# Gated scores transposed and added onto the turned probabilities, sine products of both halves in one, NF4 compares in rows of 171

## What is computed

```
qs = softmax(q); ks = softmax(k); g = log_sigmoid(k) / 16
o_lin: S = S * exp(g_t) + k_t v_t^T ; o_t = q_t S        # a scan over tokens
y = softmax(rope(q) rope(k)^T / sqrt(D), window of two blocks of 64) v
o = (0.5 * y + 0.5 * o_lin).bfloat16 @ Wo
x = x + layernorm(o)
nf4(w): per block of 64, absmax; normalized = w / (1 if absmax == 0 else absmax)
        idx = searchsorted(15 bounds, normalized); CODE[idx] * absmax
h = silu(x dq(w1)^T) * (x dq(w2)^T);  x = x + layernorm(h dq(w3)^T)
```

## Time and profile before

| | |
|---|---|
| median of 3 runs | 1913.04 us (1912.93 to 1913.94) |
| the profiled execution | 1912.8 us, its span 1911.0 us |
| PE busy | 1834.3 us, 96% |
| PEld busy | 1212.8 us, 63% |
| DVE busy | 1484.2 us, 78% |
| ACT busy | 1278.5 us, 67% |
| POOL busy | 1264.8 us, 66% |
| HBM | 47 GB/s over the span |

### The profile page before, as it was taken

The page is one execution under the profiler, slowest core; times in us unless marked ns, Lnnn a source line. Parts: engine busy times, 40 slices in busy tenths (PEclk is TensorE's granted clock), DMA queues, the critical chain, the costliest instruction groups (busy, mean ns, idle before and its releaser), DMA issues.

```text
span 1911.0 us, 42834 instructions
## 1 busy us (share of the span) xinstructions
PE 1834.3 (96%) x11439; PEld 1212.8 (63%) x11439; DVE 1484.2 (78%) x3980; ACT 1278.5 (67%) x4967; POOL 1264.8 (66%) x1164
## 2 busy tenths in 40 slices
PE   4899999999999999999999999999989999999997
PEld 3567667676777677667767776776666654444443
DVE  5999899999999888899998889999999956302112
ACT  5688777777777777777777777777677745312121
POOL 2767777777777777777777777777766738212121
PEclk8999999999999999999999999999999999999999
DMA  6101111111111111111111111111211033000000
GB/s 223 54 30 44 38 50 48 46 44 46 45 45 43 43 48 43 43 43 43 43 44 50 43 43 43 43 43 35 85 31 30 24 110 111 34 1 22 0 22 22
DMA packets 85452, 90.51 MB, mean 47 GB/s; under 512 B 14216, under 2 KB 56456, under 8 KB 85384
## 3 DMA queue, kind: packets, MB, share of 16 engines
q1 hardware_dynamic: 85384, 89.71, 15.2%
HBM read 76.48 MB, written 13.18 MB: 47 GB/s over the span
## 4 chain that ended last, share of the span: by engine, by line
PE 49%; DVE 23%; issue 19%; POOL 4%; ACT 2%; DVEq 1%; DMA 0%; POOLq 0%; ACTq 0%
PE bank L1369 12%; PE bank L1398 6%; PE bank L1358 5%; DVE f_s L1061 5%; PE bank L1340 4%; PE bank L1414 4%; PE bank L1496 3%; PE bank L1407 3%; PE bank L1435 3%; DVE f_nrm L1048 2%; PE bank L1324 2%; DVE qtT L961 2%; POOL hl L600 2%; PE bank L1514 2%; DVE qc L909 2%
## 5 line engine op out<-in xcount | busy, mean ns | idle before, releaser
L554 POOL TENSOR_TENSOR f_acc<-f_acc,f_s 128x512 f32<-128x512 f32 x429 | 548.9, 1279 | 32.6 <-POOL f_acc L554 0.4
L1369 PE MATMUL bank<-wh,xh 128*128 (+2 forms) x1024 | 335.0, 327 | 7.5 <-DVE cumh L1210 6.3
L1369 PE MATMUL bank<-wl,xh 128*128 (+2 forms) x1024 | 335.0, 327 | 0.0
L1369 PE MATMUL bank<-wh,xl 128*128 (+2 forms) x1024 | 334.8, 327 | 0.0
L1061 DVE TENSOR_SCALAR f_s<-f_nrm 128x512 f32<-128x512 f32 x480 | 282.1, 647 | 3.5
L538 POOL TENSOR_TENSOR pr<-pr,rp 128x512 f32<-128x512 f32 x128 | 133.3, 1041 | 216.1 <-DVE rp L983 216.1
L651 ACT ACTIVATE qe<-bank,nqm 128x128 f32<-128x128 f32 x512 | 180.9, 365 | 95.7 <-DVE qs L912 84.0
L1496 PE MATMUL bank<-xh,w 128*128 (+3 forms) x704 | 218.4, 379 | 1.7 <-ACT sg L837 1.7
L600 POOL TENSOR_TENSOR hl<-hf,hh 128x512 f16<-128x512 f32 (+1 forms) x44 | 51.3, 1167 | 231.4 <-ACT hh L843 231.4
L1220 DVE SCALAR_TENSOR_TENSOR hf<-bank,sg 128x512 f32<-128x512 f32 (+1 forms) x44 | 30.3, 689 | 221.5 <-PE bank L1496 210.6
L1358 PE MATMUL bank<-wh,oT 128*128 (+1 forms) x512 | 194.0, 379 | 4.4 <-DVE xl L1127 3.6
(11 more groups left out here) (179 smaller groups left out, 4918.9 us busy)
## 6 DMA issues: line engine op xcount, KB each, us to landing
f_blk<-wa SPq DMA_DIRECT2D x33, 320.0 KB, 2.9
f_raw<-wb SPq DMA_DIRECT2D x33, 256.0 KB, 2.7
dequantised<-f_w SPq DMA_DIRECT2D x33, 256.0 KB, 2.0
w<-dequantised SPq DMA_DIRECT2D x33, 256.0 KB, 4.3
raw_qkv<-wq SPq DMA_DIRECT2D x29, 256.0 KB, 2.4
raw_o<-wo SPq DMA_DIRECT2D x29, 256.0 KB, 2.6
f_recb<-scales SPq DMA_DIRECT2D x99, 64.0 KB, 2.6
f_absb<-scales SPq DMA_DIRECT2D x99, 64.0 KB, 2.6
```

What stands on the lines that cost most here:

```text
L554: nc.gpsimd.tensor_tensor(f_acc[:], f_acc[:], f_s[:, step, :], ALU.add).then_inc(s["f_ad"], 1)
L1369: last = nc.tensor.matmul(dst, av, w[:, sl + c, lo:hi], start=(n == 0), stop=(n == 3 * NC - 1))
```

## The change

Six edits:

1. **Scores.** `probabilities(l2)` now stands ahead of `gla_scores(l2)` on PE, right behind `project_out`, and opens the accumulation in `X1`. `gla_scores` has no mask matmuls: it multiplies with the keys as the stationary operand, so that the scores come out transposed, and adds them onto the turned probabilities, in two f32 matmuls of 256 columns. The first of them (queries 0 to 63 of the tile) needs only the first 64 keys; they are in a new tile `ktF`, whose other columns stay zero, and ACT's `copy_ktT` writes it with one more instruction, behind a wait for the scores of the tile before.
2. **Mask.** `cau` is now 0 or 1; `merge` is one product of the bank with `cau`, straight into `pa`. `copy_pa` on ACT is gone, and DVE's `merge` stands behind `add_out`.
3. **State.** The product `em` on DVE and its semaphore are gone; ACT's `decays` makes `em` with one exponential of one column, with a bias of 0 or -1e30, in turns with p = 0 of the tile.
4. **Sine.** `rope` has one sine product over both halves, read from the bank in reversed order of the halves.
5. **NF4.** `f_s` has rows of 171 columns at a pitch of 172; `f_nrm` and `f_acc` have 3 x 171 = 513 columns without a gap. The zero-maximum guard `f_safe` is gone: each block has a 65th column with the smallest normal number, so the maximum is never zero.
6. **`nf4_end`** stands behind `p_max` instead of ahead of `gla_k`. So POOL's first addition of a piece, which waits for it, and ACT's `nf4_high`, which is queued ahead of `p_exps`, are released later.

Around it: two more memsets on DVE at the start, `cum` moves into the space of `f_s`, and the block maxima's load is 65/64 as long.

```
-                half = lambda a: a.rearrange("p (h n) -> p h n", h=GRP)[:, 0:2, 0:WIN]
-                nc.tensor.matmul(half(X1[:]), identb[:], half(cau[:]), start=True, stop=False)
-                nc.tensor.matmul(X1[:, 2 * P:], identb[:], cau[:, 2 * P:], start=False, stop=False)
...
+                for b, keys in enumerate((ktF[:], ktT[:, r, :])):
+
+                    last = nc.tensor.matmul(X1[:, b * 256:(b + 1) * 256], keys,
+                                            qtT[:, r, b].rearrange("p h n -> p (h n)"),
+                                            start=False, stop=(b == 1), skip_group_check=True)
...
 def probabilities(t):
-                wait_tile(pe, s["pm_d"], t)
+                wait_tile(pe, s["pn_p"], t)
+                wait_tile(pe, s["pa_ev"], t, 1)
                 for j in range(GRP):
-                    last = nc.tensor.transpose(X1[:, j * P:(j + 1) * P], pr[:, r, j * P:(j + 1) * P], ident[:])
+                    last = nc.tensor.matmul(X1[:, j * P:(j + 1) * P], pr[:, r, j * P:(j + 1) * P], ident[:],
+                                            start=(j == 0), stop=False, is_transpose=True, skip_group_check=True)
...
 def merge(t):
-                nc.vector.scalar_tensor_tensor(out=half(v), in0=half(X1[:]), scalar=0.0, in1=half(v),
-                                               op0=ALU.max, op1=ALU.add)
-                nc.vector.scalar_tensor_tensor(out=v[:, 2 * P:], in0=X1[:, 2 * P:], scalar=0.0, in1=v[:, 2 * P:],
-                                               op0=ALU.max, op1=ALU.add).then_inc(s["pm_d"], 1)
+                nc.vector.tensor_tensor(pa[:, t.p % 2, :], X1[:], cau[:], ALU.mult).then_inc(s["pa_ev"], 1)
...
 def copy_ktT(t):
                 wait_tile(act, s["ktT_done"], t)
+                wait_tile(act, s["at_done"], t, 1)
+                nc.scalar.activation(ktF[:, 0:WIN], SM[:, 0:WIN], ACT.Copy)
                 nc.scalar.activation(ktT[:, t.p % 2, :], SM[:, 0:P], ACT.Copy).then_inc(s["ktT_ev"], 1)
...
-                nc.vector.tensor_tensor(d4[:, :, 0, :], s4[:, :, 1, :], sin_b(t, 0, n), ALU.mult)
-                nc.vector.tensor_tensor(d4[:, :, 1, :], s4[:, :, 0, :], sin_b(t, 1, n), ALU.mult).then_inc(done, 1)
+                nc.vector.tensor_tensor(d4, s4[:, :, ::-1, :], sin_b(t, n), ALU.mult).then_inc(done, 1)
...
-                    nc.vector.tensor_scalar(f_s[:, k % 8, :], f_nrm[:], float(BOUND[k]), float(DELTA[k]),
+                    nc.vector.tensor_scalar(step_rows(k % 8), in_rows(f_nrm[:]), float(BOUND[k]), float(DELTA[k]),
                                             ALU.is_gt, ALU.mult).then_inc(s["f_sd"], 1)
...
-                    nc.gpsimd.tensor_tensor(f_acc[:], f_acc[:], f_s[:, step, :], ALU.add).then_inc(s["f_ad"], 1)
+                    nc.gpsimd.tensor_tensor(in_rows(f_acc[:]), in_rows(f_acc[:]), step_rows(step), ALU.add).then_inc(s["f_ad"], 1)
```

More of the change, by code:

```diff
@@ L38 @@
 BLK = 64
+GUARDED = BLK + 1
+SMALLEST = float(np.finfo(np.float32).tiny)
 NF4_PIECE = 512
+NF4_ROWS = 3
+NF4_ROW = 171
 NF4_MAXIMA = 10
@@ L204, in layer @@
         ktT = sb("ktT", [P, 2, P])
+        ktF = sb("ktF", [P, P])
         krT = sb("krT", [P, 4, WIN])
@@ L218, in layer @@
         rp = sb("rp", [P, 2, GRP])
-        f_safe = sb("f_safe", [P, NF4_MAXIMA])
         PQ, PKV, X0, X1, SC, SM, PO, PW = bank
@@ L550, in add_step @@
                         pool.wait_ge(s["f_dqd"], j)
[L551 removed]
+                    nc.gpsimd.tensor_tensor(in_rows(f_acc[:]), step_rows(first), step_rows(step), ALU.add).then_inc(s["f_ad"], 1)
                 elif k > 1:
                     pool.wait_ge(s["f_ad"], j * 14 + (k - 1))
[L554 removed]
+                    nc.gpsimd.tensor_tensor(in_rows(f_acc[:]), in_rows(f_acc[:]), step_rows(step), ALU.add).then_inc(s["f_ad"], 1)
             def nf4_add(t):
@@ L664, in decays @@
                 nc.scalar.activation(edT[:, r, :], SM[:, P:P + 130], ACT.Exp)
+                if t.p == 0 and not (isinstance(t.i, int) and t.i == 0):
+                    nc.scalar.activation(em[:, 0, :], SM[:, 2 * P:2 * P + 1], ACT.Exp,
+                                         bias=keep[:].unsqueeze(2)[:, t.i % 2, :])
                 nc.scalar.activation(ked, ked, ACT.Exp, scale=-1.0).then_inc(s["dec_ev"], 1)
@@ L795, in turn @@
                         split_high(0, job, 3)
-                if l2.real():
-                    copy_pa(l2)
                 if x_tile_at(n):
@@ L865, in _ @@
             silu(0, 0)
-            copy_pa(l1)
             high_hidden(0, 0)
@@ L900, in _ @@
             nc.vector.memset(krT[:], 0.0).then_inc(s["z_id"], 1)
+            nc.vector.memset(f_nrm[:], 0.0)
             nc.vector.memset(f_col[:], 0.0).then_inc(s["z_id"], 1)
+            nc.vector.memset(ktF[:], 0.0).then_inc(s["z_id"], 1)
             cos_b = lambda t, n: cos[:, t.i % 2, t.p, :].unsqueeze(1).to_broadcast([P, n, P // 2])
-            sin_b = lambda t, half, n: sin[:, t.i % 2, t.p, half, :].unsqueeze(1).to_broadcast([P, n, P // 2])
+            sin_b = lambda t, n: sin[:, t.i % 2, t.p, :, :].unsqueeze(1).to_broadcast([P, n, 2, P // 2])
             def rope(t, src, n, dc, ds, done):
@@ L1075, in nf4_end @@
                     dve.wait_ge(s["f_lod"], j)
-                nc.vector.scalar_tensor_tensor(out=f_dq[:], in0=f_acc[:], scalar=float(CODE[0]), in1=f_absb[:],
+                nc.vector.scalar_tensor_tensor(out=f_dq[:], in0=f_acc[:, 0:NF4_PIECE], scalar=float(CODE[0]), in1=f_absb[:],
                                                op0=ALU.add, op1=ALU.mult).then_inc(s["f_dqd"], 1)
@@ L1140, in turn @@
                     q_sums(l1)
-                if t.p == 1 and not (isinstance(t.i, int) and t.i == 0):
-                    nf4_end(t.i - 1)
                 if t.p == 2 and not (isinstance(t.i, int) and t.i == 0):
@@ L1154, in turn @@
                     p_max(l1)
+                if t.p == 1 and not (isinstance(t.i, int) and t.i == 0):
+                    nf4_end(t.i - 1)
                 log_decay(t)
@@ L1330, in gla_scores @@
                 wait_tile(pe, s["ktT_ev"], t)
-                wait_tile(pe, s["pa_ev"], t, 1)
-                half = lambda a: a.rearrange("p (h n) -> p h n", h=GRP)[:, 0:2, 0:WIN]
-                nc.tensor.matmul(half(X1[:]), identb[:], half(cau[:]), start=True, stop=False)
-                nc.tensor.matmul(X1[:, 2 * P:], identb[:], cau[:, 2 * P:], start=False, stop=False)
-                for b in range(2):
-                    keys = (b + 1) * WIN
-                    for hp in range(2):
-                        j = 2 * b + hp
-                        last = nc.tensor.matmul(X1[:, j * P:j * P + keys],
-                                                qtT[:, r, b, 2 * hp:2 * hp + 2, :].rearrange("p h n -> p (h n)"),
-                                                ktT[:, r, 0:keys], start=False, stop=(j == 3))
+                for b, keys in enumerate((ktF[:], ktT[:, r, :])):
+                    last = nc.tensor.matmul(X1[:, b * 256:(b + 1) * 256], keys,
+                                            qtT[:, r, b].rearrange("p h n -> p (h n)"),
+                                            start=False, stop=(b == 1), skip_group_check=True)
                 last.then_inc(s["at_done"], 1)
@@ L1588, in constants @@
     win = np.ascontiguousarray(win.reshape(P, 2, 512))
-    n = np.arange(P)[:, None] % WIN
-    cau = np.zeros((P, 2, 2, P), np.float32)
-    for b in range(2):
-        cau[:, b] = np.where(n + b * WIN >= slot, 0.0, -3e38)[:, None, :]
+    key = np.arange(P)[:, None]
+    query = np.arange(WIN)[None, :]
+    cau = np.zeros((P, 2, GRP, WIN), np.float32)
+    cau[:, 0] = ((key >= WIN) | (query >= key))[:, None, :]
+    cau[:, 1] = (query + WIN >= key)[:, None, :]
     cau = np.ascontiguousarray(cau.reshape(P, 512))
@@ L1602, in constants @@
     cum /= 16.0
-    keep = np.ones((P, 2), np.float32)
-    keep[:, 0] = 0.0
+    keep = np.zeros((P, 2), np.float32)
+    keep[:, 0] = MASKED
     return {"cosc": cos, "sinc": sin, "winmask": win, "causal": cau, "cumsum": cum,
```

78 lines of the change are left out of this document (34 added, 44 removed).

## The result

The changed kernel takes **1844.14 us** (median of 4 runs, 1843.49 to 1844.88) against 1912.99 (4 runs, 1912.75 to 1913.94) before: ratio **0.9639**, 95% interval 0.9623 to 0.9656, or 68.8 us less.

A forecast was written before the change was run, and what follows sets the result against it. PE was taken as the bound, with 60 us of stalls waiting for DVE, whose instructions wait for POOL. PE -24, steady stalls -20, start and end -10: -54, from 1912.8 to 1859 us; own range 1848 to 1868, 8-in-10 range 1845 to 1880.

The forecast's parts named there:

- PE's own work: On PE, mask matmuls removed and scores slightly cheaper: each turn 0.19 us shorter, -24 us over 127 turns.
- The stall before the scores: PE's wait for `qtT`, 0.43 us per four turns: 1.5 us of room from cheaper compares, so it goes.
- The stall before the update: PE's wait for `kt` ahead of the state update: of 0.69 us per four turns 0.25 is left.
- Start and end: Stalls in the first and last turns, 19 + 14.5 us: 30% of 34 gained, -10 us.
- The tail: What follows the turns: the forecast's sum has no term for it.
- Dearer compares elsewhere: DVE in turns with p = 0, 1, 2: compares add up to 0.5, 1.0, 1.2 us, hidden under PE.
- `em` and the merged sines: DVE: without `em` (0.87 us) `p_max` is no longer late; merged sines save 0.06 before `qtT`, 0.1 before `kt`.
- Rival A: Stalls only exchanged, through late `oT`, `ktT` or `qtT`: 1884 us, or between 1868 and 1884; chance 0.17.
- Rival B: DVE's compares still take the two-element form, 3.67 us for four: about 1862 us; counted within the forecast's chance of 0.66.
- C: More gained: no stall in steady turns, most gone at both ends, 1843 us; chance 0.10 with all below 1848.
- D: POOL becomes the bound, its additions in rows of 171 taking up to 1.93 us: about 1985 us; chance 0.05.

The follow-up runs named there:

- e7: Changed kernel with `nf4_end` back at its old place ahead of `gla_k` instead of behind `p_max`: 1854.84 us, ratio 0.9697.
- e3: Changed kernel with compares and additions on one run of 512 columns instead of rows of 171: 1884.38 us, ratio 0.985.
- e6: Changed kernel with the sine product in `rope` as two instructions again, for q and for k: 1847.48 us, ratio 0.9658.
- e15: Changed kernel with compares and additions on runs of 512, and five of POOL's additions cut to 256 columns: 1843.75 us, ratio 0.9639.
- e11: Changed kernel with one more DVE instruction in every turn, a repeated row maximum of q ahead of `rope`: 1895.20 us, ratio 0.9904.
- e5: Changed kernel with the product `em` back on DVE instead of ACT's exponential: 1844.60 us, ratio 0.9644.
- e8: Kernel before with one edit only, compares and additions in 3 rows of 171: 1904.92 us, ratio 0.9961.
- e13: Changed kernel with compares and additions on runs of 512, plus one DVE instruction ahead of the four compares in turns with p = 3: 1885.13 us, ratio 0.9853.
- e1: Kernel before with only the edits on scores and mask: 1902.18 us, ratio 0.9945.
- e10: Changed kernel with the gap in the compares' source `f_nrm`, while `f_s` and `f_acc` are without gap: 1847.98 us, ratio 0.9659.

## Why the prediction was right or wrong

The mechanism was right for the steady turns: PE's shorter work, and a stall before the scores that goes because the compares no longer wait. The forecast is 15 us too high because three terms of its sum were sized too small: "of 0.69 I leave 0.25" for the stall before the update (6 us), "I take 30% of 34" for the stalls at start and end (5 us), and nothing for the tail (3 us).

- **PE's own work, -24:** right. 11.285 became 11.093, 127 turns x 0.19 = 24.4. The scores cost 0.87, as taken from `output`.
- **The stall before the scores:** right, gone, for the reason given: four compares in 2.46 (I had 2.4) with nothing to wait for.
- **The stall before the update:** mis-sized, by 6 us. I worked out that `kt` comes 0.3 to 0.5 earlier and is wanted 0.25 later, 0.55 to 0.75 against a stall of 0.69, and still left 0.25 for `kt` and for ACT's copy of `PO`. Nothing is left. `kt` does come 0.36 earlier, counted from the turned key (982.41 - 978.30 before, 940.87 - 937.12 now):

```profile
982.41 0.35 DVE L951 SCALAR_TENSOR_TENSOR kt<-ke,rks,bank 128x128 f32<-128x128 f32 x1
```

```profile
940.87 0.35 DVE L952 SCALAR_TENSOR_TENSOR kt<-ke,rks,bank 128x128 f32<-128x128 f32 x1
```

But the 0.69 was not all `kt`'s, as PE and PEld of the kernel before show for that turn:

```profile
981.63 1.02 PE L1414 MATMUL bank<-qtT,sr 128*128 128x512 f32 x2
982.81 0.49 PE L1417 MATMUL bank<-va,kt 128*128 128x128 f32 x2 [0.15 <-DVE kt L951]
983.35 0.66 PE L1407 MATMUL bank<-ident,pr 128*128 128x128 f32 x4
```

```profile
983.34 0.42 PEld L1407 LDWEIGHTS bank<-ident,pr 128*128 128x128 f32 x4 [0.24 <-DVE pr L993]
```

In the turn without a stall the state's matmuls and the update start 0.86 apart (947.34, 948.20), and the update and the turn of `pr` 0.22 (948.20, 948.42). Here it is 1.18 and 0.54: 0.32 of stall at `kt` and 0.32 up to `pr`, for which the weight load waits until `merge` is done. The second wait goes with the move of that turn, whatever `kt` does; against the first stand 0.36 + 0.25 = 0.61. With `nf4_end` back at its place (e7) 0.41 of its 0.58 returns, so the room now is 0.17. The allowance for ACT had no row behind it, and PE never waits for `oT`.
- **Start and end, 30% of 34, -10:** mis-sized, -15 after PE's share (stalls of 19 became 10, of 14.5 became 8.5). I had no row for the 30%. The table of e3 shows where it comes from: without the rows, start and end take 200.4 and 171.2 where the changed kernel takes 193.1 and 165.6, so 12.9 of the 15 us hang on the rows. The sines give some 3 of it (e6, 1.5 and 1.6 by the traces); such shares overlap and don't add up.
- **The tail, nothing:** it gave 2.9. The late compares stand there as well, but it isn't their form alone: e15 has them over runs of 512 and its tail takes 385.5, as the changed kernel's 385.4. The cause stays open.
- **Dearer compares elsewhere stay under cover:** right, but my rooms of 0.4 and 0.7 for single turns were the wrong picture. DVE has some 0.9 a step, in all (e11), and 0.17 ahead of `kt` in one turn (e7).
- **`em` and the merged sines:** in the steady turns worth nothing next to the rows (e5, e6). No run undoes the guard.
- **Rival A, the stalls only exchanged:** it did not come, PE waits for nothing in the steady turns. But exchange is what half of the change gives: in e3 the stall for `kt` is gone and the one for `qtT` is 1.04, in e8 the one for `qtT` is gone and the one for `kt` is 1.02, against 1.12 for both before.
- **Rival B was priced wrong, by 22 us, the largest error,** though the time didn't turn on it. I wrote that 3.67 us would stay where it is and that the time would be about 1862; it is 1884 (e3). The step that failed there: "the stall before `qtT` shrinks by 0.25 + 0.06 all the same". I took a compare's wait as a fixed price. It is a meeting with POOL: compares that start 0.6 earlier wait 0.6 longer, and end 0.62 behind the last addition (e13). So much saved on DVE ahead of them is lost, and counted from the turned key the last addition ended 0.95 us ahead of it before (966.58 - 965.63) and 0.14 ahead in e3 (720.33 - 720.19), so `qtT` is later in the turn by nearly 0.8. Of that 0.19 is the shorter turn; why POOL's queue is 0.6 later was not traced. The moved `nf4_end` is not needed for it: e1 has it at its old place, and its five additions stand as late in the turn.
- **C, at 0.10, came within 1 us,** in part by luck: it took 20 off start and end, where it is 15, and nothing off the tail, where it is 3. The low end of 1845 was too high: it cut off the one case in which DVE's edits remove all steady stalls.
- **D:** refuted, in the other direction. An addition in rows is 0.13 shorter. That may be worth something: e10, with long ones, is 3.8 us slower by the medians, about the least that two medians tell, and by its trace all of it is in start (196.59 against 193.09) and end.

So the 68.8 us are 24 of PE's own work, 41 of stalls in the turns, and 3 behind them. The rows alone give 8, the other edits without rows 28.7, and 24 of these are PE's own work: each removes one stall, and the other one grows. The sum of the two is 37; the other 32 come only with both.

## What to carry to other kernels

If a DVE instruction waits for POOL, don't give it a fixed price: look at when POOL's last instruction beside it ends, and count from there. Before you choose the faster form of an instruction, ask what it waits for; here the form that is slower when undisturbed (0.60 against 0.36) is worth 40 us, and it is bought with one unused column in 172. Two edits that each disappoint alone can be worth more than their sum if the loop has two stalls and each edit removes one while the other grows, so undo edits one by one from the full version, not only add them one by one. And measure slack over the whole period of the loop, by an added instruction: here DVE was busy 92% of a step and 0.9 us from being the bound.
